# One layer's expert results returned to their tokens by adding scatters in memory, and its place masks halved

## The reference, cut to what matters

```python
logits = xf @ Wr + br                      # xf: layernorm(x), 2048 x 256
Sm = jax.nn.softmax(logits, axis=-1)
G_t, idx_t = jax.lax.top_k(Sm.T, k)        # k = 2048 // 8 = 256 tokens per expert
G, idx = G_t.T, idx_t.T
tokens = xf[idx]
mid = jax.nn.silu(jnp.einsum('keh,ehf->kef', tokens, Wu) + bu)   # f = 682
out = jnp.einsum('kef,efh->keh', mid, W_down) + b_down
y = jnp.zeros_like(xf).at[idx].add(G[..., None] * out)
x = x + y
x = x + L2_xattn(layernorm(x), ...)        # the layer that follows
```

## Time and profile before

| what | value |
|---|---|
| three timed runs, median (lowest, highest) | 4020.46 us (4018.89, 4025.84) |
| the profiled execution, its own time | 4023.51 us |
| its span in the trace | 4021.8 us |
| mean granted TensorE clock | 0.946 of full speed |
| TensorE busy with matmuls | 3619.9 us, 90% of the span |
| VectorE, ScalarE, GpSimd busy | 2136.0, 1240.4, 885.5 us |
| chain that ended last: TensorE's share | 73% |

### The profile page before, as it was taken

The page is one execution under the profiler, slowest core; times in us unless marked ns, Lnnn a source line. Parts: engine busy times, 40 slices in busy tenths (PEclk is TensorE's granted clock), DMA queues, the critical chain, the costliest instruction groups (busy, mean ns, idle before and its releaser), DMA issues.

```text
span 4021.8 us, 90691 instructions
## 1 busy us (share of the span) xinstructions
PE 3619.9 (90%) x38548; PEld 2738.2 (68%) x38548; DVE 2136.0 (53%) x5317; ACT 1240.4 (31%) x3136; POOL 885.5 (22%) x1360
## 2 busy tenths in 40 slices
PE   7988547988994989999999989999999999998996
PEld 6866445546773776877777646668777777776774
DVE  6756623354456355555555466654444456665346
ACT  6852101232210213333333343322222244443111
POOL 6666042021000333222222232300000010102002
PEclk9989678999995999999999999999999999999997
DMA  5610156251001211111111100012211111111000
GB/s 166 180 41 4 34 201 228 91 184 43 3 3 60 68 50 48 46 46 47 45 48 48 51 1 2 3 61 84 72 60 58 59 38 38 38 38 54 2 2 25
DMA packets 197906, 238.29 MB, mean 59 GB/s; under 512 B 17956, under 2 KB 179360, under 8 KB 194560
## 3 DMA queue, kind: packets, MB, share of 16 engines
q1 hardware_dynamic: 191552, 201.03, 16.3%
q0 software_dynamic: 5952, 31.46, 2.3%
HBM read 219.42 MB, written 12.64 MB: 58 GB/s over the span
## 4 chain that ended last, share of the span: by engine, by line
PE 73%; DVE 11%; issue 9%; ACT 3%; POOL 3%; DMA 1%; SPq 0%; ACTq 0%; POOLq 0%; DVEq 0%
PE psum L180 48%; PE psum L3294 10%; PE psum L888 2%; DVE l3x_P L3626 2%; PE psum L860 1%; PE psum L2730 1%; PE psum L3522 1%; PE psum L2831 1%; PE psum L2799 1%; DVE g_xn L243 1%; DVE l3x_V L3609 1%; PE psum L873 1%; POOL l0a_ms L1072 1%; PE psum L2740 1%; PE psum L2731 1%
## 5 line engine op out<-in xcount | busy, mean ns | idle before, releaser
L230 POOL TENSOR_SCALAR g_rs<-g_mv 128x4 f32<-128x4 f32 x40 | 17.1, 428 | 1063.1 <-DVE g_mv L278 1062.0
L3294 PE MATMUL psum<-l2f_hhi,l2f_whi 128*128 128x512 f32 x512 | 200.9, 392 | 0.0
L3294 PE MATMUL psum<-l2f_hlo,l2f_whi 128*128 128x512 f32 x512 | 199.2, 389 | 0.0
L3294 PE MATMUL psum<-l2f_hhi,l2f_wlo 128*128 128x512 f32 x512 | 199.2, 389 | 0.0
L180 PE MATMUL psum<-l2x_kT,l2x_Qp 128*128 128x257 f32 x768 | 179.2, 383 | 2.6 <-ACT g_xn L3190 2.6
L180 PE MATMUL psum<-g_xn,l2x_tok 128*128 128x384 f32 x512 | 177.7, 489 | 1.4 <-ACT g_xn L3199 1.4
L180 PEld LDWEIGHTS psum<-l2x_kT,l2x_Qp 128*128 128x128 f32 x768 | 142.0, 191 | 21.7 <-issue 3.0
L3340 DVE CAST l2f_hhi<-l2f_tmp 128x512 fp32r<-128x512 f32 x96 | 40.9, 427 | 202.1 <-ACT l2f_tmp L3398 201.0
L289 DVE TENSOR_TENSOR g_x<-g_x,psum 128x256 f32<-128x256 f32 x144 | 60.0, 417 | 161.3 <-PE psum L180 158.8
L180 PEld LDWEIGHTS psum<-g_xn,l2x_tok 128*128 128x128 f32 x512 | 93.3, 190 | 56.9 <-issue 2.6
L3609 DVE COPY l3x_V<-psum 128x512 f32<-128x512 f32 x64 | 44.3, 692 | 159.1 <-PE psum L180 159.1
(11 more groups left out here) (738 smaller groups left out, 9355.2 us busy)
## 6 DMA issues: line engine op xcount, KB each, us to landing
l2f_raw<-L2f_h SPq DMA_DIRECT2D x64, 512.0 KB, 3.5
l0x_ctxT<-ctxT SPq DMA_DIRECT2D x64, 257.0 KB, 2.8
l1x_ctxT<-ctxT SPq DMA_DIRECT2D x64, 257.0 KB, 5.7
l0x_ctok<-ctx SPq DMA_DIRECT2D x64, 256.0 KB, 3.1
l1x_ctok<-ctx SPq DMA_DIRECT2D x64, 256.0 KB
l2x_cT<-ctxT SPq DMA_DIRECT2D x64, 256.0 KB, 2.7
l2x_tok<-ctx SPq DMA_DIRECT2D x128, 128.0 KB, 2.9
l3x_ctxT<-ctxT SPq DMA_DIRECT2D x64, 256.0 KB, 2.7
```

The lines of the kernel that those rows point to most:

```text
L3294: t = e.matmul(z, a, b, start=c == 0 and u == 0, stop=c == 7 and u == 2)
```

## The change

It touches `l1_ffn` alone, and the DRAM buffer it uses is declared beside the others.

- The return to the tokens is done in memory. SP stores x to a DRAM buffer `acc` in one DMA of 2 MB behind the stores of `xs`. After each expert GpSimd issues two indirect DMAs of 128 rows that add `yf` to rows of `acc` (`add`), each pair after the pair before has landed. When all 16 have landed, SP reads `acc` back into x in four DMAs of 512 KB, and VectorE takes the statistics of each tile. The masks `ohT`, the 512 matmuls, `y`, `yl` and the additions to x are gone. `yf` has four buffers in place of two.
- The place is split into its half of the list and its place in that half (`half`, `lo`). The mask has 128 columns in place of 256; it becomes the weights of `ids`, and 6 columns (`inf2`: three numbers for either half) move past. The result comes out with the places on the partitions, so the copy to `idc` and `turn_ids` are gone. The cast to `idi` comes ahead of the gate's sum. The unused fourth column of `info` is gone.

```diff
--- before.py
+++ after.py
...
-        info, gf = T("info", [128, 8, 16, 4], F32R), T("gf", [128, 8, 16])
-        sa, sb, rk = T("sa", [128, 8, 16]), T("sb", [128, 8, 16]), T("rk", [128, 8, 16])
-        oh, ohT = [T(f"oh{k}", [128, 16, 256], F32R) for k in range(2)], [T(f"ohT{k}", [128, 16, 128], F32R) for k in range(2)]
-        gid, idi, idr = T("gid", [128, 16, 4]), T("idi", [128, 16], I32), T("idr", [128, 16])
+        info, inf2, gf = T("info", [128, 8, 16, 3], F32R), T("inf2", [128, 8, 16, 2, 3], F32R), T("gf", [128, 8, 16])
+        sa, sb, rk, lo, half = T("sa", [128, 8, 16]), T("sb", [128, 8, 16]), T("rk", [128, 8, 16]), T("lo", [128, 8, 16]), T("half", [128, 2, 8, 16])
+        oh = [T(f"oh{k}", [128, 16, 128], F32R) for k in range(2)]
+        gid, idi = T("gid", [128, 16, 3]), T("idi", [128, 16], I32)
         X, XT = [T(f"x{k}", [128, 256]) for k in range(4)], [T(f"xT{k}", [128, 2, 256]) for k in range(2)]
...
-        y, yl = T("y", [128, 16, 256], F32R), T("yl", [128, 16, 256], F32R)
...
@@ -2353,8 +2352,13 @@
             for g in range(4):
                 w.wait_ge(norm.xn.at(4 * g + 4))
                 load(e, xs_in, xnd[:, 4 * g:4 * g + 4, :], xn[:, 4 * g:4 * g + 4, :])
+            load(e, sum_in, A["acc"].rearrange("(i p) d -> p i d", p=128), x[:])
             for n in range(3, 8):
                 expert(n)
+            w.wait_ge(added.at(16))
+            back = A["acc"].rearrange("(i p) d -> p i d", p=128)
+            for g in range(4):
+                load(e, back_in[g], x[:, 4 * g:4 * g + 4, :], back[:, 4 * g:4 * g + 4, :])
 
...
-                matmuls(e, z[0:4, 0:256], [(info[:, n, i, :], oh[n % 2][:, i, :]) for i in range(16)]).then_inc(*id_ps.up())
-
-            def turn_ids(n):
-                w.wait_ge(idc_ok.at(n + 1))
-                for u in range(2):
-                    t = e.transpose((bank[0], bank[7])[n % 2][:, 256 + 4 * u:260 + 4 * u], idc[:, n % 2, u * 128:(u + 1) * 128],
-                                    K.ident[0:4, 0:4])
-                t.then_inc(*idT_ps.up())
+                matmuls(e, z[:, 0:6], [(oh[n % 2][:, i, :], inf2[:, n, i].rearrange("p u v -> p (u v)")) for i in range(16)]).then_inc(*id_ps.up())
 
...
-            ticks(8, {1: ids, 2: turn_ids, 3: turn, 4: up, 5: down}, order)
-
-            def add(i):
-                w.wait_ge(y_ok.at(16))
-                w.wait_ge(ohT_ok.at(i + 1))
-                if i >= 2:
-                    w.wait_ge(xs.at(i - 1))
-                matmuls(e, bank[5 + i % 2][:, 0:256], [(ohT[i % 2][:, s // 2, :], (y, yl)[s % 2][:, s // 2, :])
-                                                       for s in range(32)]).then_inc(*back_ps.up())
-
-            ticks(16, {1: add}, [1])
+            ticks(8, {1: ids, 3: turn, 4: up, 5: down}, order)
 
...
-            for s in range(16):
+
+            def fetch(n):
                 w.wait_ge(xs_in.at(4))
-                w.wait_ge(idi_ok.at(s // 2 + 1))
-                if s >= 4:
-                    w.wait_ge(turned.at(s - 3))
-                e.indirect_dma_start(X[s % 4][:], None, A["xs"], bass.IndirectOffsetOnAxis(idi[:, s:s + 1], 0)).then_inc(*x_in[s % 4].up())
+                w.wait_ge(idi_ok.at(n + 1))
+                for s in range(2 * n, 2 * n + 2):
+                    if s >= 4:
+                        w.wait_ge(turned.at(s - 3))
+                    e.indirect_dma_start(X[s % 4][:], None, A["xs"], bass.IndirectOffsetOnAxis(idi[:, s:s + 1], 0)).then_inc(*x_in[s % 4].up())
+
+            def add(n):
+
+                w.wait_ge(sum_in.at(1))
+                w.wait_ge(yf_ok.at(2 * n + 2))
+                if n >= 1:
+                    w.wait_ge(added.at(2 * n))
+                for s in range(2 * n, 2 * n + 2):
+                    e.indirect_dma_start(A["acc"], bass.IndirectOffsetOnAxis(idi[:, s:s + 1], 0), yf[s % 4][:], None,
+                                         compute_op=ALU.add).then_inc(*added.up())
+
+            ticks(8, {3: fetch, 6: add}, [3, 6])
 
...
-            e.tensor_copy(info[:, :, :, 3], tno[:].unsqueeze(1).to_broadcast([128, 8, 16]))
             w.wait_ge(router.sel_ok.at(1))
             e.tensor_tensor(gf[:], sel[:], router.probs[:], ALU.mult).then_inc(*step.up())
             w.wait_ge(step.now())
             e.tensor_copy(info[:, :, :, 1], gf[:]).then_inc(*step.up())
             w.wait_ge(step.now())
-            e.tensor_tensor(info[:, :, :, 2], gf[:], info[:, :, :, 1], ALU.subtract).then_inc(*info_ok.up())
+            e.tensor_tensor(info[:, :, :, 2], gf[:], info[:, :, :, 1], ALU.subtract).then_inc(*step.up())
             before(e, w, step, sel, sa, sb, pre)
             e.tensor_scalar(rk[:], sel[:], -4096.0, 4096.0, ALU.mult, ALU.add).then_inc(*step.up())
             w.wait_ge(step.now())
@@ -2463,49 +2463,45 @@
             e.tensor_tensor(rk[:], rk[:], bank[1][:, 0:128].rearrange("p (e i) -> p e i", e=8), ALU.add).then_inc(*step.up())
             w.wait_ge(step.now())
 
+            e.tensor_scalar(lo[:], rk[:], 128.0, -128.0, ALU.is_ge, ALU.mult)
+            e.tensor_scalar(half[:, 0], rk[:], 128.0, None, ALU.is_lt)
+            e.tensor_scalar(half[:, 1], rk[:], 256.0, None, ALU.is_lt).then_inc(*step.up())
+            w.wait_ge(step.now())
+            e.tensor_tensor(lo[:], lo[:], rk[:], ALU.add)
+            e.tensor_tensor(half[:, 1], half[:, 1], half[:, 0], ALU.subtract).then_inc(*step.up())
+            w.wait_ge(step.now())
+            for u in range(2):
+                t = e.tensor_tensor(inf2[:, :, :, u, :], info[:], half[:, u].unsqueeze(3).to_broadcast([128, 8, 16, 3]), ALU.mult)
+            t.then_inc(*info_ok.up())
+
             def places(n):
                 if n >= 2:
                     w.wait_ge(id_ps.at(n - 1))
-                e.tensor_tensor(oh[n % 2][:], rk[:, n, :].unsqueeze(2).to_broadcast([128, 16, 256]),
-                                iota[:].unsqueeze(1).to_broadcast([128, 16, 256]), ALU.is_equal).then_inc(*oh_ok.up())
+                e.tensor_tensor(oh[n % 2][:], lo[:, n, :].unsqueeze(2).to_broadcast([128, 16, 128]),
+                                iota[:, 0:128].unsqueeze(1).to_broadcast([128, 16, 128]), ALU.is_equal).then_inc(*oh_ok.up())
 
             def ids(n):
                 sl = slice(2 * n, 2 * n + 2)
-                w.wait_ge(idT_ps.at(n + 1))
-                e.tensor_copy(gid[:, sl, :].rearrange("p s n -> p (s n)"), (bank[0], bank[7])[n % 2][:, 256:264]).then_inc(*gid_ok.up())
+                w.wait_ge(id_ps.at(n + 1))
+                e.tensor_copy(gid[:, sl, :].rearrange("p s n -> p (s n)"), (bank[0], bank[7])[n % 2][:, 0:6]).then_inc(*gid_ok.up())
                 w.wait_ge(gid_ok.now())
+                e.tensor_copy(idi[:, sl], gid[:, sl, 0]).then_inc(*idi_ok.up())
                 e.tensor_tensor(gid[:, sl, 1], gid[:, sl, 1], gid[:, sl, 2], ALU.add).then_inc(*step.up())
-                e.tensor_copy(idi[:, sl], gid[:, sl, 0]).then_inc(*idi_ok.up())
 
             def down(n):
                 w.wait_ge(y_ps.at(n + 1))
                 w.wait_ge(step.now())
+                if n >= 2:
+                    w.wait_ge(added.at(2 * n - 2))
                 for u in range(2):
                     s = 2 * n + u
-                    e.tensor_scalar(yf[u][:], bank[5 + n % 2][:, u * 256:(u + 1) * 256], gid[:, s, 1:2], None,
+                    e.tensor_scalar(yf[s % 4][:], bank[5 + n % 2][:, u * 256:(u + 1) * 256], gid[:, s, 1:2], None,
                                     ALU.mult).then_inc(*yf_ok.up())
-                    w.wait_ge(yf_ok.now())
-                    e.tensor_copy(y[:, s, :], yf[u][:]).then_inc(*step.up())
-                    w.wait_ge(step.now())
-                    e.tensor_tensor(yl[:, s, :], yf[u][:], y[:, s, :], ALU.subtract).then_inc(*y_ok.up())
 
             ticks(8, {0: places, 2: ids, 5: down}, order)
-            e.tensor_copy(idr[:], gid[:, :, 0]).then_inc(*step.up())
-
-            def back(i):
-                if i >= 2:
-                    w.wait_ge(back_ps.at(i - 1))
-                w.wait_ge(step.now())
-                e.tensor_tensor(ohT[i % 2][:], idr[:].unsqueeze(2).to_broadcast([128, 16, 128]),
-                                iota[:, 0:128].unsqueeze(1).to_broadcast([128, 16, 128]), ALU.is_equal).then_inc(*ohT_ok.up())
-                w.wait_ge(ohT_ok.now())
-                e.tensor_scalar(idr[:], idr[:], -128.0, None, ALU.add).then_inc(*step.up())
-
-            def total(i):
-                w.wait_ge(back_ps.at(i + 1))
-                add_x(K, e, i, bank[5 + i % 2][:, 0:256])
-
-            ticks(16, {0: back, 1: total}, [0, 1])
+            for i in range(16):
+                w.wait_ge(back_in[i // 4].at(1))
+                statistics(K, e, w, i)
 
...
-            def ids(n):
-                w.wait_ge(id_ps.at(n + 1))
-                if n >= 2:
-                    w.wait_ge(idT_ps.at(n - 1))
-                copy_act(e, idc[:, n % 2, :], (bank[0], bank[7])[n % 2][0:4, 0:256]).then_inc(*idc_ok.up())
 
...
```

(24 more changed lines are left out.)

## The result

The changed kernel takes 3971.94 us (median of four; 3969.84 to 3974.81), the kernel before beside it 4022.6 (4018.89 to 4025.84). The ratio is 0.9876, with a 95% interval of 0.9864 to 0.9889: some 51 us faster, between 45 and 55. The forecast was 3964.5, in a range of 3956 to 3978.

The account below looks back on a forecast made before the run. The prediction took the uncovered 69.3 us tail between the last expert's product and the last statistics as the target: -52.2 + 2.0 - 3.8 - 2.0 = -56.0 us, hence 3964.5 us against the median, range 3956 to 3978.

Parts of the forecast that it names:

- The issue of two scatters: Tail, GpSimd after the last product: two adding scatters priced at 1.0 each like plain ones, 2.6 us with gaps.
- The landing, 3.2: Tail, from the last scatter to the read-back: 3.2 us, two times the plain scatter's 1.6; bounds 1.6 and 9.4.
- Read-back and statistics, 10.4: End of tail: four 512 KB loads, the last landing at 8.6, then 1.8 for four tiles' statistics; 10.4 us.
- The cover of the weights, 1.7 us: Next layer's weights behind the read-back: there after about 15 us, wanted by TensorE at 16.7; covered by 1.7.
- The front, +2.0 and -3.8: Before the experts: +2.0 us of VectorE work ahead of the first mask, then -3.8 to the first transposes.
- The ticks, -2.0: Expert ticks: -1.6 us without `turn_ids`, -0.4 from the sums of ids at the low clock; -2.0 in all.
- The weights of `ids` at full clock, 0.12 a load: Sums of ids in the ticks: bound by 128-column weight loads, 0.12 us each, so 2.0 us as before.
- GpSimd and VectorE inside the ticks: Expert ticks of 14 us: scatter pairs of some 6 to 9 us and the waits for them stay covered.
- the slow addition: Rival on the tail: addition slow but shorter than a tick, 8 us more, late weights up to 5; 3973 to 3978; chance 0.18.
- The chain of scatters that outlasts the ticks: Rival on the ticks: serial pairs set the end, slower than before from 19.3 us a pair; chance 0.03.
- Cheap weights of 0.06: Rival on the ids: 0.06 us a load gives 5.0 less, an escaping second gather 1.8 less; 3958; chance 0.12.
- the front gives nothing back: Rival on the front: the shorter mask falls on the same gather, 3.8 us missing; 3968; chance 0.66 together with the forecast.

Follow-up runs that it names:

- e4_plain_scatter: The changed kernel with plain, overwriting scatters in place of adding ones, so the sum is left out; 3970.27 us in one run.
- e3_weights_held: The changed kernel, with SP waiting for all four read-backs before it issues the next layer's weights; 3985.58 us in one run.
- e6_D_first: The changed kernel, with GpSimd building the next layer's matrices D ahead of the norm's roots; 3968.83 us, ratio 0.9862 to the kernel before.
- e7_weights_first: e6_D_first, with the next layer's value and key weights also issued ahead of the read-back, after the last gated results; 3964.04 us, ratio 0.9851.
- e11_all: The changed kernel with matrices ahead of the roots, value and key weights issued earlier, and both groups of filling matmuls; 3958.5 us, ratio 0.9844.

## Why the prediction was right, and by how much its terms were off

Direction, size and mechanism held: what takes the tail's place is not covered by anything, and it is all of the gain but two or three microseconds. The sum was -56.0; in the trace it is -52.7. The missing 3.3 are these terms:

- *The issue of two scatters, "Between once and twice that time for each, I take once": wrong, 1.1 short.* From the first issue to the second's end it is 3.42 for 2.3. An adding scatter takes 1.56, 1.6 times the plain 0.97, and `e4_plain_scatter` shows that the addition alone is the reason.
- *The landing, 3.2: 0.9 too much.* It is 2.27; 1.5 times the plain one of 1.46 in the same place. That this error and the one above nearly cancel is luck.
- *Read-back and statistics, 10.4: 1.8 short.* They take 12.19. The row I took stood alone; here 1.6 MB of weights follow from the same engine, and that is 0.5 to 1.4 of it (`e3_weights_held`). I had reckoned those weights against their own lateness only, and not against the transfer in front of them.
- *The tail as a whole:* 1.15 + 3.42 + 2.27 + 12.19 = 19.03 for 17.1.
- *The cover of the weights, 1.7 us:* it held, and was wider. With D ready at once (`e6_D_first`) TensorE is held 1.81 behind the statistics, so that of D's 6.2 us some 4.4 were cover.
- *The front, +2.0 and -3.8:* +2.00 and -3.21. The step's mechanism held: the masks took 2.28, and the first two gathers 2.45 and 2.95 beside them, against 0.94 alone. Too small was the time of the first ids, 3.56 for 3.1, 0.22 a load in place of 0.19. The row of the 0.19 was misread: its granted clock is 0.59, so that part of those 69 loads ran at full clock, and "at its low clock" holds for the rest alone.
- *The ticks, -2.0: they gave -1.15.* The steady ticks did what was said, 13.64 for 14.00; from the first tick on they gained 2.1. The first lost 0.95, and this step failed in what it held constant: "one at the low clock gives -0.4" changes the sums alone and leaves the clock's rise where it was. In the trace that rise comes some 3 us later behind the same transposes, and the 24 up-matmuls pay for it. How late it comes changes from execution to execution, and -2.0 would have been right for the earliest of the nine (`e4_plain_scatter`, -1.9).
- *TensorE's longer rest before the next layer costs nothing:* so it was. Its first weight loads there start 0.64 apart again, until 1444.0, and queries follow 33.9 later as before.
- *The weights of `ids` at full clock, 0.12 a load:* 1.79 from their start to the next matmul (1314.81 to 1316.59), 0.112. The Trainium skill ("TensorE: Matmul & The Clock Gate", LDWEIGHTS) leads to an estimate of 0.107, which this row bears out better than my own value. A load of 128 columns lasts longer than one of 4 (0.192 for 0.085), but nothing is lost by it: the 16 sums take 1.93 where they took 2.00 with 256 columns moving past.
- *GpSimd and VectorE inside the ticks:* no stretch of the chain between 1303 and 1413 waits for a scatter. TensorE's first product of the next layer waits for D, as forecast. None of the signs of being wrong appears: the landing is 2.27 and the steady ticks are 13.64.

Against the measured median the forecast was 7.4 too low: 3.3 are the terms above; the median of before is 2.1 higher with its fourth run (4022.6); the other 2 are within what the later layers differ by from execution to execution.

Of the rivals, the slow addition was half true: dearer than the plain scatter, by 2.0 a pair and not by the 8 that it needed. The chain of scatters that outlasts the ticks fell by a factor of three. (Its 1423 leaves out the forecast's own -3.8 up to there; with it the bound is 19.0 and not 19.3.) Cheap weights of 0.06 fell with the 0.112, and the second gather did not escape the mask; that the front gives nothing back fell with the -3.21.

## What to carry to other kernels

When a computed return (masks and matmuls) is replaced by memory traffic, price it by the chain: issue, landing, read-back; only the last item's pass through it counts as long as a pair is shorter than the work that makes the next one. Price a transfer with what is queued behind it, too. And when such a tail is gone, look at what starts after it but doesn't depend on it: here weights and a constant matrix, moved ahead, brought the next layer's queries another 14 us forward. Of the 11.9 that `e7_weights_first` has of this in the trace, its timed runs show 9.

## What the runs showed of the hardware

- An indirect scatter of 128 rows of 1 KB takes GpSimd 0.97 us when it overwrites and 1.56 when it adds; from its start to its landing 2.4 and 3.8. Two weight loads beside it make the latter 5.9.
- Replacing 4-column weights with 256 columns moving past by 128-column weights with 6 moving past leaves the sums' time nearly the same (2.00 and 1.93), but behind them the granted clock rose 6.5 to 9.8 us after the second transposes in nine executions, and 4.4 and 4.8 in the two with 256 columns moving past. A pause of 0.19 us was all that lay between ids at 1.92 and the same ids at 3.48; in `e11_all`, the same program up to there, the second ids took 1.95. What decides this stays open.
